# Idle matmuls in the second batch's slots of a batched attention and mixture-of-LoRA kernel, and a new list of full slots

## What is computed

```python
def _L0_attn_ref(x, w_in, b_in, w_out, b_out):
    ...
    x_proj = (x @ w_in.T + b_in).reshape(b, l, h, -1)
    q, k, v = jnp.split(x_proj, 3, axis=-1)
    att = jnp.einsum('blhd,bmhd->blmh', q, k) * scale
    att = jax.nn.softmax(att, axis=2)
    opt = jnp.einsum('blmh,blhd->blhd', att, v).reshape(b, l, d)
    return opt @ w_out.T + b_out
...
    top1 = jnp.argmax(jax.nn.softmax(logits, axis=-1), axis=-1)
    base = jnp.einsum('bsd,fd->bsf', x, wi_W) + wi_b
    for i in range(lora_A.shape[0]):
        lora = jnp.einsum('bsr,fr->bsf', jnp.einsum('bsd,rd->bsr', x, lora_A[i]), lora_B[i])
        inter = jax.nn.relu(base + lora)
        expert_out = jnp.einsum('bsf,df->bsd', inter, wo_W) + wo_b
        mask = (top1 == i).astype(x.dtype)[..., None]
        out = out + mask * expert_out
...
    x = x + _layernorm(_L0_attn_ref(_layernorm(x, axis=-1), ...), axis=-1)
    x = x + _layernorm(_L0_ffn_ref(_layernorm(x, axis=-1), ...), axis=-1)
```

## Time and profile before

| | us |
|---|---|
| median of 3 runs | 548.2 (547.74 to 549.51) |
| the profiled execution, device time | 549.36 |
| its span, first to last instruction | 547.6 |
| PE busy | 518.1 (95%) |
| ACT busy | 457.8 (84%) |
| DVE busy | 459.9 (84%) |
| POOL busy | 332.6 (61%) |
| mean granted clock of TensorE | 0.976 |

### The profile page before, as it was taken

The page is one execution under the profiler, slowest core; times in us unless marked ns, Lnnn a source line. Parts: engine busy times, 40 slices in busy tenths (PEclk is TensorE's granted clock), DMA queues, the critical chain, the costliest instruction groups (busy, mean ns, idle before and its releaser), DMA issues.

```text
span 547.6 us, 8941 instructions
## 1 busy us (share of the span) xinstructions
PE 518.1 (95%) x2785; PEld 418.2 (76%) x2785; DVE 459.9 (84%) x987; ACT 457.8 (84%) x1242; POOL 332.6 (61%) x504
## 2 busy tenths in 40 slices
PE   8988977899999999999999999999999998998995
PEld 6756635577887788787987788787878776767995
DVE  4499888797999989998999899998999889893453
ACT  2499987899989998999989998999899988894230
POOL 8794043414980699339971798159942985597262
PEclk9989988599999999999999999999999999999999
DMA  6493353006230544017220625044401740310011
GB/s 247 144 243 97 101 132 77 1 1 173 69 107 1 132 100 135 20 43 189 68 89 1 159 73 154 1 115 117 115 1 31 186 132 0 78 38 2 1 40 39
DMA packets 22535, 47.24 MB, mean 86 GB/s; under 512 B 5237, under 2 KB 13557, under 8 KB 21848
## 3 DMA queue, kind: packets, MB, share of 16 engines
q1 hardware_dynamic: 21800, 45.56, 31.4%
q10 hardware_dynamic: 432, 0.59, 0.3%
q0 software_dynamic: 256, 0.52, 0.3%
HBM read 7.85 MB, written 4.19 MB: 22 GB/s over the span
## 4 chain that ended last, share of the span: by engine, by line
PE 48%; POOL 29%; ACT 10%; DVE 6%; issue 4%; DMA 1%; SPq 0%; POOLq 0%; DVEq 0%
PE pu L193 26%; PE ps L222 10%; ACT ps L519 8%; POOL y L1018 6%; POOL nmr L1012 5%; POOL inter L1078 4%; PE ps L193 4%; POOL xb L1024 4%; POOL vo L1055 3%; DVE nmax L738 2%; POOL xn L1018 2%; PE pu L227 2%; POOL inter L1076 2%; PE pu L314 2%; POOL nmr L1010 2%
## 5 line engine op out<-in xcount | busy, mean ns | idle before, releaser
L519 ACT ACTIVATE ps<-ps,nmax 128x512 f32<-128x512 f32 x512 | 343.9, 698 | 24.7 <-DVE nmax L738 24.1
L738 DVE TENSOR_REDUCE nmax<-ps 128x1 f32<-128x512 f32 x512 | 321.2, 681 | 34.4 <-PE ps L222 33.8
L222 PE MATMUL ps<-stack 128*128 128x512 f32 x512 | 176.2, 422 | 11.3 <-ACT ps L519 9.4
L222 PEld LDWEIGHTS ps<-stack 128*128 128x128 f32 x512 | 93.4, 193 | 49.5 <-ACT ps L519 34.5
L519 ACT ACTIVATION_READ_ACCUMULATOR ps<-ps,nmax 128x1 f32 x512 | 125.0, 244 | 0.0
L193 PE MATMUL pu<-yT,wi_r 128*128 128x512 f32 x336 | 87.8, 397 | 0.0
L193 PE MATMUL pu<-wo_r,inter 128*128 128x256 f32 x648 | 85.3, 285 | 0.0
L193 PEld LDWEIGHTS pu<-wo_r,inter 128*128 128x128 f32 x648 | 81.0, 189 | 1.5
L193 PEld LDWEIGHTS pu<-yT,wi_r 128*128 128x128 f32 x336 | 62.9, 189 | 13.6
L1032 POOL TENSOR_TENSOR ml<-gs,g 128x128 f32<-128x128 f32 (+1 forms) x9 | 3.6, 402 | 104.2 <-DVE g L878 104.2
L1078 POOL TENSOR_TENSOR inter<-y,inter 128x1024 fp32r<-128x1024 f32 x26 | 62.0, 2386 | 2.1
(11 more groups left out here) (150 smaller groups left out, 684.7 us busy)
## 6 DMA issues: line engine op xcount, KB each, us to landing
stack<-qk SPq DMA_DIRECT2D x256, 128.0 KB, 2.5
xb<-in_x SPq DMA_DIRECT2D x7, 512.0 KB, 3.6
out_y<-xb SPq DMA_DIRECT2D x7, 512.0 KB, 3.6
xb<-in_wo SPq DMA_DIRECT2D x1, 1024.0 KB, 5.9
vo<-in_wi SPq DMA_DIRECT2D x2, 512.0 KB, 5.8
oT<-in_wqk ACTq DMA_DIRECT2D x1, 512.0 KB, 4.1
xb<-in_x SPq DMA_DIRECT2D x4, 128.0 KB, 4.1
stack<-qk SPq DMA_DIRECT2D x8, 64.0 KB, 2.1
```

What stands on the lines that cost most here:

```text
L222: e.matmul(ps[i % NS][:], st[:, 1 - p, c, t * 128:(t + 1) * 128], st[:, 2, c, :], start=True, stop=True).then_inc(scored, 1)
L519: e.activation(ps[i % NS][:], ps[i % NS][:], ACT.Exp, bias=nmax[:, i % 8:i % 8 + 1], accum_out=ssum[:, b % 2, t, h:h + 1]).then_inc(exped, 1)
L738: e.tensor_reduce(nmax[:, i % 8:i % 8 + 1], ps[i % NS][:], AX_X, ALU.max, negate=True).then_inc(maxed, 1)
```

## The change

The condition in `pair` now reaches over the slots of both batches, and `FULL` is another list. In the first batch slots 16 and 18 to 21 lose their idle matmuls (ten), and slots 7, 8, 12, 13, 27, 28 and 30 get them (fourteen); slot 15 stays without. In the second batch slots 32, 33, 38, 39, 41 to 46, 54, 58 and 60 get them (twenty-six), the other nineteen have none. All in all TensorE has thirty matmuls more. No other engine's list changes.

```diff
--- before.py
+++ after.py
@@ -18,7 +18,8 @@
 XB = 5
 PAIRS = 32
 
-IDLE, FULL = (25, 6, 4), (7, 8, 12, 13, 15, 27, 28, 30)
+IDLE, FULL = (25, 6, 4), (15, 16, 18, 19, 20, 21, 34, 35, 36, 37, 40, 47, 48, 49, 50, 51, 52, 53, 55, 56, 57,
+                           59, 61, 62, 63)
 NS = 5
 GATE_STEPS, MASK_STEPS = 10, 4
 CONSTS, LATE = 12, 22
@@ -216,7 +217,7 @@
                     i = 2 * g + p
                     if i >= NS:
                         e.wait_ge(exped, i - NS + 1)
-                    if 2 <= g < PAIRS + 2 and g - 2 not in FULL:
+                    if 2 <= g < 2 * PAIRS + 2 and g - 2 not in FULL:
                         run_idle(ps[i % NS], 1)
                     st = stack[:, piece % PIECES]
                     e.matmul(ps[i % NS][:], st[:, 1 - p, c, t * 128:(t + 1) * 128], st[:, 2, c, :], start=True,
```

## The result

| | before | after |
|---|---|---|
| median of 11 runs, us | 548.67 (547.63 to 550.20) | 545.74 (543.89 to 547.76) |
| ratio | | 0.9938, 95% interval 0.9921 to 0.9955 |
| the profiled execution, device time | 549.36 | 544.66 |
| its span | 547.6 | 542.9 |
| its mean granted clock | 0.976 | 0.997 |

A forecast was written before the change was run, and what follows sets the result against it. TensorE was taken to bound 46 to 62 us and from 122 on, ScalarE 62 to 74.5, with two half-clock holes between; -1.5 - 1.1 - 1.1 + 0.46 + 1.4 = -1.8 off 548.2 gave 546.3 us, range 543.5 to 548.8.

The forecast's parts named there:

- likeliest case: Whole kernel: removal gains, both clock holes shrink to falls of about 3.3 us; 545.3 to 547.4 us, chance 0.48.
- a sign of being wrong: Start of the second batch: a clock full from 78 to 109 us would show the prediction wrong.
- the rival in which both holes close: Clock full through 78 to 85 and 103 to 109 us: -4.7, 543.5 us; chance 0.25 for one or both.
- The removal: First batch, 46 to 62 us: ten idle matmuls gone give back ScalarE's gaps, 0.36 + 0.65 + 0.53 = 1.5 us.
- The idle matmuls put at nothing: Eighteen in slots 7 to 33, where ScalarE has the work, and fourteen beside GpSimd's run (38, 39, 41 to 45): no cost.
- The first hole: Low clock, 78.0 to 84.9 us: gain 1.1 us, bounds 0 and 2.5; a short fall in the projections costs 1.0 to 1.7.
- The second hole: Low clock, 95.1 to 108.8 us, paid only from 103.39: gain 1.1 us, bounds 0 and 2.6; short falls expected.
- Slots 54, 58 and 60: Six added idle matmuls in 121 to 132 us, where TensorE has no gap: 1.4 us lost, lower bound 0.5.
- Holes stay as they are: Rival: both low stretches at the second batch's start keep their length; +0.8, 549.0 us, chance 0.14.
- The removal brings nothing: Rival: ScalarE's gaps in 46 to 62 us belong to VectorE, so 1.5 us goes; 547.8 us, chance 0.08.
- Slower, idle matmuls at half clock ahead of the fourth projection: Rival: clock still low at slots 38 and 39, after 86.9 us, delays the last projection; +2.8, 551.0 us, chance 0.05.
- The transposes: Transposes of v and y: not counting as clock activity, they make falls certain; if they count, 1 us more may be gained.

The follow-up runs named there:

- e0: The changed kernel measured again, nothing else altered: 545.76 us, 0.9936 of the kernel before.
- e5: The changed kernel without the idle matmuls of slots 27, 28, 30, 32 and 33: 546.01 us, 0.9938 of the kernel before.
- e2: The changed kernel with the ten idle matmuls of slots 16 and 18 to 21 kept: 546.29 us, 0.9945 of the kernel before.
- e4: The changed kernel's list for the first batch, with no idle matmul added in the second: 546.72 us, 0.9958 of the kernel before.
- e1: The kernel before with only the ten idle matmuls of slots 16 and 18 to 21 taken away: 547.39 us, 0.9950 of the kernel before.
- f4: e7 with the added idle matmuls of both f1 and f2: 542.65 us, 0.9875 of the kernel before.
- e3: The changed kernel without the six idle matmuls of slots 54, 58 and 60: 544.38 us, 0.9908 of the kernel before.
- e6: The changed kernel with, of the second batch's added idle matmuls, only those of slots 32 and 33: 544.51 us, 0.9920 of the kernel before.
- e7: The changed kernel without the idle matmuls of slots 46, 54, 58 and 60: 543.92 us, 0.9895 of the kernel before.
- f2: e7 with four more idle matmuls in the last batch's slots 11 and 12, ahead of its transposes of y: 544.10 us, 0.9900 of the kernel before.
- f3: The changed kernel with idle matmuls in every slot of the second batch, 38 more: 550.52 us, 1.0022 of the kernel before.
- f1: e7 with thirteen idle matmuls where TensorE waits in the second batch: 543.58 us, 0.9891 of the kernel before.

## Why the prediction was right, and where not

The forecast was 546.3 us, and the median is 545.74, inside the range and inside the likeliest case's own range (545.3 to 547.4). It was forecast as more likely faster than not, and faster by 0.6% it is.

The time is right, but the mechanism of its likeliest case is not what the profile shows. That case had two low stretches of some 3.3 us between 78 and 109 us, and a clock that is full there was named as a sign of being wrong. It is full there in the profiles of after, e0 and e5. The profiled execution is the rival in which both holes close. The nearness of the median to 546.3 is in part luck, as the sum below shows. The steps:

**The removal** was put at 1.5 us. It is 1.33 to 1.39 in every trace that has it, and absent in e2. The mechanism, that ScalarE's gaps are what comes back and not the 2.3 us of TensorE, is as put: the gaps are gone. Two of the three losses came back in full (0.36 and 0.53); the one at the eviction of v gave 0.45 to 0.50 and not 0.65. The prediction had noted that 0.92 us of idle matmuls stood there against 1.01 to be won, and counted all of it.

**The idle matmuls put at nothing** cost nothing: in after the lead of ScalarE's exps stays at -0.22 to -0.21 from 24 to 50 us, where slots 7 to 13 run, and at 1.12 to 1.13 from 60.89 to 73 us, where 27 to 30 do. Slots 38 and 39 and 41 to 45 run beside GpSimd, as the rows said.

**The first hole.** The bound, 2.5 us with the hole closed, was good: in after the lead grows by 2.25 from 60.89 to the transposes of y. The expectation for a short fall, 1.0 to 1.7 lost, was good too: e4 lost some 1.5. What failed is the reasoning for which of them comes. The prediction argued from idle matmuls on both sides of a gap, one trace, one hole. e1 has the hole closed without any of the added ones, e5 with none in the run-up, e4 has a short one with the run-up: in single executions it is open.

**The second hole.** "103.39 to 108.54, 5.15 at half clock and 2.6 at full" is 2.79 in f4 and 3.23 with the two idle matmuls of slot 46 (0.44 for them, 0.46 was put). With a short fall it is 4.80 (e3). The free part ahead of it is free: with the clock low from 93.8 (e6) and from 90.2 us (e1) the lead grows by 2.4 from the exp behind the v products to the transposes of y, no less than the 2.25 of after, where it is full. What failed is again the forecast that falls come here: not in after, e0 and e5, but in e2, e3, e7 and f2, one short one each. Against the path without a fall it cost 1.4 to 1.6 us, up to 1.7 was put.

**Slots 54, 58 and 60** were mis-sized. The term was 6 x 0.23 = 1.4, with "no slack takes the delay up". TensorE did lose 1.03 of it by the close of the batch (the lead went from 5.41 to 4.38). A few microseconds later, where GpSimd takes over the chain, 0.9 is left of the loss. Here is the same operation of GpSimd before and after:

```profile
141.94 2.39 POOL L1078 TENSOR_TENSOR inter<-y,inter 128x1024 fp32r<-128x1024 f32 x1
...
137.47 2.39 POOL L1079 TENSOR_TENSOR inter<-y,inter 128x1024 fp32r<-128x1024 f32 x1
```

The lead is 4.47 there, and it stays at 4.5 to 200 us. The loss is 0.91 to 0.94 in after, e0, e2 and e5, and none in the kernels without the six. So the term is 0.9 and not 1.4, 0.15 for each matmul. f3 says about the same with 38 of them: 0.12 to 0.16 each. Why less than 0.23 is paid was not measured; small waits inside a stretch that the busy time shows as full, which an idle matmul fills, would do it.

**Sum.** With both holes closed the prediction had -4.7 us for the profiled execution, and it was 549.36 to 544.66, -4.70. That agreement is luck: the late slots were put 0.5 too dear and the removal and the two holes together 0.5 too good, and the later start (0.2) is made up by 0.2 that the kernel after gains between 200 us and the end, where the lists are the same. In the median it is -2.9 where -1.9 was forecast. (The terms add up to -1.84, which from 548.2 gives 546.4, not 546.3.)

The rest lies between the cases: the case with falls and the case without are no alternatives between which the kernel decides once, but executions of one kernel. The prediction gave them chances of 0.48 and 0.25 as if one of them were true. Of the eleven executions of after three have at most 3.3 us at half clock and take 543.9 to 544.7 us; the other eight have 6.5 to 9.8 and take 545.4 to 547.8. Where the low stretches of those eight lie was not profiled. In the profiles of the kernels near it they lie at the transposes of y, which was foreseen as possible, and at 455 us, which was not.

**The rivals.** "Holes stay as they are" is out (26 us at half clock before, 7 after). "The removal brings nothing" is out by the traces. "Slower, idle matmuls at half clock ahead of the fourth projection" was not seen in any profile; in none was the clock low past that point in the first hole.

**The transposes.** The Trainium skill, "TensorE: Matmul & The Clock Gate", Part 4, says that transposes do not count as activity for the clock. The prediction read from it that the falls were certain, and they are not: in after, e0 and e5 the clock stays at 1.00 through the same transposes of v and y. Nor do the transposes of y always stand ahead of a fall. It began 0.5 us behind the start of the first of them in e3 (100.6 us) and 0.1 behind it in f2 (99.8), but 0.4 us before it in e2 (100.4, the transpose at 100.75) and in e7 (99.5, the transpose at 99.86). There the engine was in the wait of 1.4 us ahead of them. f1 and f4, with idle matmuls in that wait, did not fall. So these runs do not show that transposes matter to the clock; a wait of 1.4 us with no fall stands in after, e0 and e5 too, and what decides in which execution it falls stays open.

## What to carry to other kernels

Where TensorE's clock falls at gaps, look for it in many executions and not in one profile: the spread of the times and the mean clock of each of them tell more than any single trace, and a version whose clock is steady shows it by a small spread (here 0.35 us in four executions, against 3.9 in 17 of the kernel before on the same chip). Price a hole by the part of it in which TensorE is on the chain, here 5 of 13 us. Put idle matmuls into the waits themselves, ahead of what is waited for and into a bank that is overwritten next; ahead of dense work they cost, here 0.12 to 0.16 us each where 0.23 is their time, and enough of them made the kernel slower than having none.

## What the runs showed that was not expected

The clock can fall where no profile so far has shown it. In five of the profiles it fell once more between 454 and 459 us, in the last round, at a gap of 1.1 us ahead of transposes, and cost 1.3 to 1.5 us; before and after had the same code there and stayed at full clock. And differences between executions, not the code, made 5 us of spread in a kernel whose median was to be judged at 1.6: of 59 executions of the kernel before the fastest took 546.5 us, which is less than the medians of e1 (547.4) and e4 (546.7).
